# V times the output weights once per head, ahead of the rounds, in packed chunks

## The reference, cut to what matters

```
x1 = x + tanh(gate) * (softmax(q k^T / 8) v @ w_out + b_out)   # q from two layer norms of x, k and v from the context
x2 = layernorm(x1)
out = x1 + (silu(x2 @ wg^T) * (x2 @ wu^T)) @ wd^T               # integer weights, scaled by 1/127
```

## Time and profile before

| | us |
|---|---|
| median of 3 runs (316.48 to 320.73) | 316.53 |
| the profiled execution | 315.11 |
| its span | 313.3 |
| TensorE busy | 295.8 (94%) |
| VectorE, ScalarE, GpSimd busy | 231.6, 170.6, 165.7 |
| moved by DMA | 23.29 MB, mean 74 GB/s |

### The profile page before, as it was taken

One profiled execution on the slowest core, in us unless ns is written; L12 is line 12 of the kernel. 1 busy time (PEld: TensorE's weight loads), 2 busy tenths in 40 slices (PEclk: granted clock), 3 DMA queues, 4 the chain that ended last, 5 costly groups with the idle time before them and its releaser, 6 DMA issues.

```text
span 313.3 us, 6353 instructions
## 1 busy us (share of the span) xinstructions
PE 295.8 (94%) x2371; PEld 272.2 (87%) x2371; DVE 231.6 (74%) x599; ACT 170.6 (54%) x325; POOL 165.7 (53%) x164
## 2 busy tenths in 40 slices
PE   6899999897987999999999999999999999999994
PEld 6898977686985999889988989898989899978984
DVE  2298887586785887878887787779787878785653
ACT  4456874657326852773486249535942782365041
POOL 2381853347853871668086619644872677035013
PEclk9999999999999999999999999999999999999999
DMA  7993163512414020102200120202020101100010
GB/s 194 385 361 98 36 213 130 180 49 100 143 55 116 0 76 33 36 1 77 65 4 27 50 67 2 74 2 67 3 75 36 33 2 41 42 27 2 0 36 35
DMA packets 16314, 23.29 MB, mean 74 GB/s; under 512 B 1634, under 2 KB 13898, under 8 KB 16282
## 3 DMA queue, kind: packets, MB, share of 16 engines
q1 hardware_dynamic: 16282, 22.85, 22.5%
HBM read 15.87 MB, written 4.62 MB: 65 GB/s over the span
## 4 chain that ended last, share of the span: by engine, by line
PE 77%; POOL 11%; DVE 3%; issue 3%; ACT 3%; DMA 2%; POOLq 0%; SPq 0%; DVEq 0%; ACTq 0%
PE ps L786 12%; PE ps L736 8%; PE ps L722 7%; PE ps L696 5%; PE ps L704 5%; PE ps L700 5%; PE ps L623 4%; PE ps L832 4%; PE ps L836 4%; PE ps L833 4%; PE ps L816 3%; PE ps L819 3%; POOL probs L1045 3%; POOL t_lo L1052 3%; PE ps L631 2%
## 5 line engine op out<-in xcount | busy, mean ns | idle before, releaser
L1045 POOL TENSOR_TENSOR probs<-probs,total 128x616 f32<-128x616 f32 x32 | 38.9, 1217 | 75.5 <-DVE total L1170 75.5
L917 ACT COPY pt<-ps 77x512 f32<-77x512 f32 x64 | 34.1, 583 | 49.1 <-PE ps L722 49.1
L1052 POOL TENSOR_TENSOR t_lo<-t_all,t_hi 128x1232 fp32r<-128x1232 f32 x16 | 45.5, 2846 | 4.7 <-ACT t_hi L942 4.7
L1061 POOL TENSOR_TENSOR h_lo<-hid,h_hi 128x256 fp32r<-128x256 f32 x42 | 30.9, 735 | 28.4 <-ACT h_hi L977 28.4
L722 PE MATMUL ps<-ident,probs 128*77 128x128 f32 x256 | 33.4, 273 | 4.0 <-POOL probs L1045 2.9
L832 PE MATMUL ps<-wo_hi,o_hi 128*128 128x256 f32 x128 | 36.4, 284 | 0.0
L833 PE MATMUL ps<-wo_lo,o_hi 128*128 128x256 f32 x128 | 36.1, 282 | 0.0
L836 PE MATMUL ps<-wo_hi,o_lo 128*128 128x256 f32 x128 | 36.0, 281 | 0.0
L1153 DVE TENSOR_REDUCE top<-ps 128x4 f32<-128x308 f32 x64 | 28.7, 472 | 9.1 <-PE ps L704 8.9
L722 PEld LDWEIGHTS ps<-ident,probs 128*77 128x77 f32 x256 | 29.5, 147 | 5.1 <-POOL probs L1045 3.6
L696 PE MATMUL ps<-t_hi,xn_hi 128*128 128x308 f32 x128 | 30.7, 321 | 0.7 <-ACT v_out L876 0.7
(11 more groups left out here) (133 smaller groups left out, 798.0 us busy)
## 6 DMA issues: line engine op xcount, KB each, us to landing
v<-v_scratch SPq DMA_DIRECT2D x8, 308.0 KB
x_ln<-in_x SPq DMA_DIRECT2D x8, 256.0 KB, 3.9
v_scratch<-v_out SPq DMA_DIRECT2D x4, 512.0 KB, 2.9
stream<-in_x SPq DMA_DIRECT2D x8, 256.0 KB, 2.7
x_rooms<-in_x SPq DMA_DIRECT2D x7, 256.0 KB, 8.6
out<-stream SPq DMA_DIRECT2D x7, 256.0 KB, 2.2
wk_raw<-in_L_xattn_w_kv SPq DMA_DIRECT2D x4, 256.0 KB, 5.3
...
```

The source lines that it names most:

```text
L917: nc.scalar.copy(pt[:, q * HB:(q + 1) * HB, t * P:(t + 1) * P], ps_p[0:K, m % 2, :].rearrange("k (h q) -> k h q", h=HB)).then_inc(pt_copie ...
L1045: nc.gpsimd.tensor_tensor(p, p, total[:, u, :].unsqueeze(2).to_broadcast([P, HG, K]), ALU.mult).then_inc(probs_done, 1)
L1052: nc.gpsimd.tensor_tensor(t_lo[:, :, cols], t_all[:, :, n, cols], t_hi[:, :, cols].bitcast(F32), ALU.subtract).then_inc(tlo_done, 1)
```

## The change

V is made transposed (jobs v0 to v7, one per pair of heads), split, and multiplied with the pair's rows of w_out: VW_h = V_h W_h for all 616 context rows, in three jobs W per pair (rows in packs of 256, 256 and 104). Each head's part is copied from PSUM to a stage buffer (A to H; even pairs use A, B and E, odd ones C, D and E, with G and H for the last) and stored to `vw_scratch` in DRAM, laid out by batch, head and context row; where a batch ends within a pack, the store is cut. For batch 0 the heads 8 to 15 go directly into `vw_first`.

A round loads the 8 x 77 = 616 rows of each half of the heads as four chunks of 128 and one of 104, 1.26 MB per batch in four transfers, and splits them. The probabilities of a unit lie side by side, so their transposes are cut into the same chunks: `T` has four transposes, `U` (new) takes the remaining 104 columns of both token tiles. `C`, `K` (ScalarE) and `L`, `Q` (VectorE) split the transposed probabilities, `VH` and `VL` the chunks of VW. The projection is then 10 chunks by three products, 30 per token tile, and there are no values any more. For units 0 and 1 (0 to 2 in round 0) the maxima are not subtracted by VectorE but given as a bias to the exponential, one per head. The feed-forward weights are transposed among the t products, where the first W_V and w_out splits are too. The first round and the start are written out in the lists; memory is laid out anew.

```diff
-    v_scratch = nc.dram_tensor("v_scratch", (CR, INNER), F32, kind="Internal").ap()
+    vw_scratch = nc.dram_tensor("vw_scratch", (B, HEADS, K, D), F32, kind="Internal").ap()
...
-PE_ORDER = "T0 S2 T1 X1T S3 V0 XT G0 G1 G2 T2 G3 S0 T3 G4 G5 V1 S1 O0 O1 D0 D1".split()
-DVE_ORDER = "LN1 M2 LN Z2 X1 M3 O0 H0 Z3 H1 H2 M0 H3 H4 O1 Z0 H5 M1 R0 Z1 R1 AG Y0 Y1".split()
-POOL_ORDER = "P2 Ta X h0 P3 B WO h1 h2 h3 h4 Tb P0 h5 P1 XS2".split()
+PE_ORDER = "T0 S2 T1 X1T XT S3 G0 G1 G2 U0 S0 G3 G4 T2 S1 T3 G5 U1 O0 O1 D0 D1".split()
+DVE_ORDER = "LN1 LN M2 X1 L0 M3 L1 H0 Z2 H1 Z3 M0 VL0 Q0 H2 L2 H3 L3 H4 Q1 Z0 M1 H5 R0 Z1 R1 AG Y0 Y1".split()
+ACT_ORDER = "VH0 C0 Ta X1 C1 X VH1 t0 E2 t1 h0 E3 Tb t2 K0 h1 t3 E0 C2 h2 t4 C3 h3 t5 K1 h4 E1 h5".split()
+POOL_ORDER = "Ta X VL1 P2 h0 P3 h1 B h2 Tb P0 h3 h4 h5 P1".split()
+PE_START = (
...
+    "t171 f7 f8 t170 t100 t110 t101 t111 FL XT.0 t121 t131 t141 t151 t161 t120 t130 t140 t150 t160 v0 v1 W00 "
+    "W01 W02 v2 IF S0.0 W10 W11 W12 S1.0 W20 W21 v3 W22 v4 S2.0 W30 W31 W32 S3.0 v5 XT.1 W40 W41 W42 W50 v6 "
+    "W51 W52 v7 W60 W62 W70 W61 W71 W72 T0.0 T1.0 S0.1 U0.0 T2.0 T3.0 U1.0 S1.1 O0.0 T0.1 O1.0 XT.2 T1.1 S2.1 "
+    "S3.1 X1T.1 S0.2 G0.1 G1.1 G2.1 U0.1 T2.1 G3.1 G4.1 S1.2 T3.1 G5.1 U1.1 O0.1 O1.1 D0.1 D1.1 "
...
+        def slot_of(i, p):
+
+            if p == 2:
+                return "H" if i == IC - 1 else "E"
+            return {(IC - 2, 1): "D", (IC - 1, 1): "G"}.get((i, p), ("AB", "CD")[i % 2][p])
...
+            def load_vw(n, g):
+                target = vw_raw if n > 0 else vw_first
+                rows_in = vw_scratch[n, g * HG:(g + 1) * HG].rearrange("h k d -> (h k) d")
+                sp.dma_start(target[:, g * GC:(g + 1) * GC - 1, :],
+                             rows_in[0:GK - REST, :].rearrange("(j p) d -> p j d", p=P)).then_inc(vw_in[g], 16)
+                sp.dma_start(target[0:REST, (g + 1) * GC - 1, :], rows_in[GK - REST:GK, :]).then_inc(vw_in[g], 16)
...
+            def store_vw(n):
+                _, i, p = jobs[n]
+                evacuated(sp, n)
+                src = stage[slot_of(i, p)]
+                for r in range(2 * p, min(2 * p + 2, RC)):
+                    for b, k, at, count in pieces(r):
+                        block_rows = src[at:at + count] if p == 2 else src[at:at + count, :, r - 2 * p, :]
...
+                        sp.dma_start(vw_scratch[b, 2 * i:2 * i + 2, k:k + count, :].rearrange("e k d -> k e d"),
+                                     block_rows).then_inc(s_stage[slot_of(i, p)], 16)
...
+            load_res(0)
+            for s in s_stage:
+                sp.wait_ge(s_stage[s], max(v for j, v in stored.items() if slot_of(*j[1:]) == s))
+            load_vw_next(1)
...
+                if kind == "W":
+                    i, p = j[1:]
...
+                    terms = ((vt_hi, wo_hi), (vt_hi, wo_lo), (vt_lo, wo_hi))
+                    for r in range(2 * p, min(2 * p + 2, RC)):
+                        m, at_d = rows(r), (r - 2 * p) * D
+                        for at, (v, w) in enumerate(terms):
+                            for e in range(2):
+                                ds = slice(e * DH, (e + 1) * DH)
+                                ins = mm(ps[0:m, banks_of(n)[e], at_d:at_d + D], v[ds, i % 2, r * P:r * P + m], w[ds, i, :],
+                                         start=at == 0, stop=at == len(terms) - 1)
...
-                for i in range(IC):
-                    if t == 0 and i % 2 == 0:
-                        pe.wait_ge(ohi_done, NU * b + i // 2 + 1)
-                    mm(o, o_hi[:, i, ts], wo_hi[:, i, :], start=i == 0, stop=False)
-                    mm(o, o_hi[:, i, ts], wo_lo[:, i, :], start=False, stop=False)
...
-                    ins = mm(o, o_lo[:, i, ts], wo_hi[:, i, :], start=False, stop=i == IC - 1)
+                for g in range(2):
+                    if t == 0:
+                        pe.wait_ge(vwhi_done, 2 * b + g + 1)
+                        pe.wait_ge(pthi_done, 6 * b + 3 * g + 3)
+                    for pt, vw in ((pt_hi, vw_hi), (pt_lo, vw_hi), (pt_hi, vw_lo)):
...
+                        for j in range(GC):
+                            m = chunk(g, j)
+                            ins = mm(o, pt[0:m, g * GC + j, ts], vw[0:m, g * GC + j, :],
...
+                    for h in range(HB):
+                        head = r * HB + h
+                        ins = nc.scalar.activation(probs[:, u, head * K:(head + 1) * K],
+                                                   ps[:, score_bank(half), h * K:(h + 1) * K], ACT.Exp,
+                                                   bias=top[:, u, head:head + 1])
...
+            def split_vw(b, g):
+                if b == 0 and g == 1:
+                    for i in (IC - 2, IC - 1):
+                        act.wait_ge(s_stage[slot_of(i, 0)], stored["W", i, 0])
+                else:
+                    act.wait_ge(vw_in[g], 32 * (b + 1 - g))
...
+                if g == 0:
+                    wait(act, proj_done, NT * b)
+                at = slice(g * GC, (g + 1) * GC)
+                nc.scalar.copy(vw_hi[:, at, :], vw_of(b)[:, at, :]).then_inc(vwhi_done, 1)
```

More of the change, by code:

```diff
@@ new lines, in last_user, with xt_bank, biased, half_of @@
+            return None
+        def xt_bank(n):
+            return (bank["XT"], 0)[n] if n < 2 else bank["XT"]
+        def biased(b, u):
+            return u in (BIASED if b > 0 else BIASED_FIRST)
+        def half_of(b, u, r):
+            return 2 * NU * b + 2 * u + r
+        def score_bank(half):
+            return SCORE_BANKS[half % len(SCORE_BANKS)] if half >= 2 * NU else FIRST_SCORE_BANKS[half % 2]
+        def count_of(kind, half):
+            return sum(biased(h // (2 * NU), h % (2 * NU) // 2) == kind for h in range(half + 1))
@@ new lines, in packed, with direct, stores_of @@
+        def packed(h):
+            out, at = [], (h % HG) * K
+            end = at + K
+            while at < end:
+                upto = min((at // P + 1) * P, end)
+                out.append((h // HG * GC + at // P, at % P, at - (h % HG) * K, upto - at))
+                at = upto
+            return out
+        def direct(i, b):
+            return b == 0 and 2 * i >= HG
+        def stores_of(i, p):
+            return sum(sum(len(packed(2 * i + e)) for e in range(2)) if direct(i, piece[0]) else 1
+                       for r in range(2 * p, min(2 * p + 2, RC)) for piece in pieces(r))
@@ L790, in last_down @@
             def last_down(general):
+                for t in range(NT):
+                    claim(B, f"D{t}")
                 for f in range(FC):
```

1026 lines of the change are left out of this document (596 added, 430 removed), and 13 rows, old and new, of tables (ACT_START, DVE_START, PE_START).

## The result

The changed kernel takes 367.83 us (median of 4 runs, 367.06 to 368.72) against 317.19 (4 runs, 316.48 to 320.73): the ratio is **1.157, 95% interval 1.148 to 1.166**. Slower, as the likeliest case said, but 43 us above the forecast and 34 above the range. (Medians leave disturbed runs out.)

What follows compares the result with a forecast made beforehand. TensorE was taken to bound the rounds and the first DMA engine's stores the prologue: 313.3 + 28 - 18.4 = 322.9 us of span, with 1.8 and 1.4 added 326, stated as 325; range 300 to 334.

Steps and rivals of the forecast that it cites:

- the likeliest case: Prologue: scratch stores pile up on the first DMA engine; 325 us in all, by itself 317 to 333, chance 0.60.
- A round on TensorE, 26.0 to 26.5: Steady round: TensorE's net saving of 3.6 us gives 26.0; with 0.5 added for waits, 26.5.
- The other engines in a round: Steady round: busy sums of VectorE 24.4, ScalarE about 19.5 and GpSimd 20.2 us, all under TensorE's 26.0.
- TensorE stays the bound on paper: Steady round: TensorE still sets its length, with 1.6 us of air over VectorE.
- the lock: Rounds: VectorE instructions on two SBUF tensors and GpSimd's exclude each other through the shared port pair, up to 2.85 us.
- a rival of 0.12: Rounds: VectorE becomes the bound, 28.5 us each; 337 with the first-engine queue, 315 without; chance 0.12.
- V starts at 45.0: Prologue: V begins at 45.0 us instead of 40.4, as weight transposes, first x and flag add 4.6.
- TensorE could be through at 80: Prologue: V 13.4, V times W_out 14.4 and four scores 6.7 us, 34.5 after 45, end TensorE's work near 80.
- The first engine's 65.3 us: Prologue stores: 1484 elements of 1 KB at 44 ns on the first DMA engine, done at 116.4 us.
- From batch 1's loads to the gate product: Prologue: loads there at 121, ScalarE's queue of 7.9 us follows, first gate product near 129.5.
- +28 for the prologue: Prologue: round 1 ends at 149 us where the kernel before ends it at 121.3, 28 us later.
- The even deal: Prologue: stores spread over all DMA engines, SyncE's issuing decides, all landed by 95; 303 us in all, chance 0.28.

Runs made afterwards that it cites:

- a1: Changed kernel, but GpSimd's subtraction Ta waits in rounds 2 to 5 until VectorE has made x1_hat and x_hat: 351.31 us (ratio 1.103).
- f1: Changed kernel plus Ta's wait, scratch as context rows, later GpSimd bias additions and an earlier load of the first residual: 334.66 us (1.056).
- g1: On f1 with SyncE's loads reordered (339.99 us): subtraction VL1 moved from GpSimd to VectorE in every round but the first; 340.57 us.
- m2: On f1: rounds' loads as four transfers, all from another input, stores of 16 rows, none of slot E; output not the reference's; 330.12 us.
- c1: Changed kernel with scratch as context rows: 52 whole stores instead of 111, 24 small loads per round instead of 4; 355.41 us (1.117).
- b1: Changed kernel with at most 8 rows per scratch store, same number of transfers, loads from another input; output not the reference's; 355.0 us, one run.
- f3: Changed kernel with only GpSimd's bias additions B.0 and B.1 later and the first residual's load earlier: 359.67 us (1.135).

## Why the prediction was wrong, step by step

Two steps failed. In a round the other engines were taken to be free because their busy time lay below TensorE's (17.6 us). In the prologue the path was put on the stores and on ScalarE's queue alone, with TensorE through at 80 and GpSimd left out (24.2 us).

- **A round on TensorE, 26.0 to 26.5: nearly right.** TensorE's own work is 26.3 to 26.4 wherever nothing meets (a1, f1, g1), where 26.0 was summed. Round 2 took 26.5, but the steady rounds of the kernels without the meeting take 27.1, so even then the 26.5 is 0.6 short.
- **The other engines in a round: the sizes right, the consequence wrong.** VectorE was put at 24.4 us (23.4 to 23.8 measured where nothing meets), ScalarE at 19.5 (18.3), GpSimd at 20.2 (21.4). But I took sums of busy time for freedom. The step that failed here is "TensorE stays the bound on paper", with the lock kept for a rival of 0.12 and a price of "up to GpSimd's 2.85". a1 shows it in four of six rounds at 3.9 each, 15.4 us in all, which is nearly all of the 17.6. The rival had the mechanism, and the sign for it ("If rounds are over 28, VectorE or a port has them") came true, but it named the wrong pair: I looked at the vw split, which is new; the meeting that counted was of an old instruction, Ta, that had been moved to the head of GpSimd's order. VectorE's vw split also meets a normalisation of GpSimd in each round, which shows in the means of the changed kernel's groups (2.02 us for the estimated 1.5; 1.45 where the same operation of GpSimd took 1.22 when alone):

```profile
L1275 POOL TENSOR_TENSOR probs<-probs,total 128x616 f32<-128x616 f32 x32 | 46.5, 1453 | 21.8 <-DVE total L1450 21.8
L1121 ACT ACTIVATE probs<-ps,top 128x77 f32<-128x77 f32 x136 | 31.3, 350 | 12.8 <-DVE top L1430 12.7
...
L1472 DVE TENSOR_TENSOR vw_lo<-vw_raw,vw_hi 128x1280 fp32r<-128x1280 f32 x7 | 14.1, 2021 | 0.0
```

  The exponentials cost less than the text took: eight in a queue take 1.85 us, 0.23 each, where 0.3 was taken and 0.25 was its lower bound. That is most of what ScalarE stays under its 19.5.
- **V starts at 45.0: 49.5.** The t products began 2 us later (26.9) and, with the weights' transposes among them, took 22.6 instead of 20.1.
- **"TensorE could be through at 80": wrong by 20.** Added up from start to start in m2, V times W_out takes 20.2 us of TensorE, not 14.4 (pairs go by at 0.12, but a job begins with one of 0.22, and part of it ran at half clock); V takes 14.7 for 13.4, the four scores 7.7 for 6.7, and 8 us are idle. With V's later start that makes the 20. This stage was not hidden behind the DMA queue: in m2, with nearly no transfer to wait for, it is still there.
- **The first engine's 65.3 us: its size not shown, and not the main cause.** The last store had landed by 129.6 rather than 116. Two things speak for the deal itself. Counted as the prediction counts them, the divisors give 2778 short packets for the changed kernel, 16 engines for each transfer 3616, and the page has 2817. And from 56 to 86.7 us, where only these stores are in flight, the DMA share is 0.57 on average and 0.78 in its fullest half microsecond, where c1's stores of 128 rows reach 1.12 (the changed kernel first, then c1):

```profile
58.50:59.00 0.50, 0.00 (x0) 0.00 (x0) 0.50 (x1) 0.00 (x0) 0.50 (x2) 1.00 0.78 184
```

```profile
57.00:57.50 0.50, 0.18 (x2) 0.00 (x0) 0.00 (x0) 0.50 (x2) 0.50 (x1) 1.00 1.12 354
```

  That fits pieces which keep to the same part of the engines; which ones these are no run tells. But the stretch was not worth what the sum put on it: c1, which spreads its stores over all 128 partitions, gained 12 us and no more, and b1, which kept the number of transfers and moved a ninth, as much. The last W jobs, put at 106, ended at 116: the copies had waited 22 us for slot E.
- **From batch 1's loads to the gate product: 8.5 forecast, 23 measured** (loads issued 129.6 to 131.4, the first gate product at 154.3). I counted ScalarE's queue alone. GpSimd's was longer: B.0 waited for a residual behind every store, and P0.1, Ta.2, B.1, P1.1, VL1.1, X.2 and Tb.2 stood behind it; x_hat then met X.2 and Tb.2 and took 4.1 us. f3 shows 8 us of this as mere order. In the forecast's own terms the first gate product is 24.8 us late: the last landing comes 13.2 behind the 116.4, and what follows it takes 11.6 more. From the gate product to the end of round 1 the forecast holds: 18.9 us, with 18.8 and some waiting forecast.
- **+28 for the prologue: 51.8 in the kernel.** m2 comes to 26.0, near the forecast but for another reason: its time is mostly the engines' own and not the transfers'. So that "slower" came true is in part luck: the queue on which the forecast rested is worth some 12 us, and m2 is 4.6% slower without it. What makes the rest: about 12 with the stores (b1, c1), 8 to 10 with the residual's order (f3; they overlap, together 18.9 in f1), 7 with what f1 still waits for (m2).
- **The even deal (0.28), faster:** refuted. Its sign, a last store landed before 100, did not come, and with the stores spread evenly (c1) the kernel is still 12% slower than before.
- **The lower end of the likeliest case, 317,** does not follow from its own terms: 42 ns takes 3 us off and rounds of 26.0 take off 3, which gives 319.

The prologue's costs do not add up as neatly as those of the rounds, and what fills m2's extra 26 us beyond TensorE's longer stage was only read from the windows, not tested.
